# A graph network on one core: places of the edges summed as rows of one bank, in three wide products a group

## The reference

```
def L0(x):                                   # edge_index = [src, dst]
    feat = concat([x[dst], x[src] - x[dst]], -1)
    messages = relu(feat @ W1 + b1) @ W2 + b2
    out = segment_max(messages, dst)         # 0 where a row has no edge
def L1(x):
    h = x + segment_sum(x[src], dst)
    h = relu(h @ W1 + b1) @ W2 + b2
    return x @ Wres + bres + h
x = layernorm(x + L0(x))
x = layernorm(x + L1(x))
```

## Time and profile before

| | |
|---|---|
| median of three runs | 1157.18 us (1156.98 to 1157.43) |
| the profiled execution | 1157.41 us, its span 1155.6 us, mean granted clock 0.981 |
| TensorE products / weight loads | 1083.7 us (94%) / 836.6 us (72%) |
| VectorE, ScalarE, GpSimd | 939.1 (81%), 896.5 (78%), 764.7 us (66%) |
| transfers | 232.04 MB, 201 GB/s over the span |

### The profile page before, as it was taken

One profiled execution on the slowest core, in us unless ns is written; L12 is line 12 of the kernel. 1 busy time (PEld: TensorE's weight loads), 2 busy tenths in 40 slices (PEclk: granted clock), 3 DMA queues, 4 the chain that ended last, 5 costly groups with the idle time before them and its releaser, 6 DMA issues.

```text
span 1155.6 us, 27075 instructions
## 1 busy us (share of the span) xinstructions
PE 1083.7 (94%) x7463; PEld 836.6 (72%) x7463; DVE 939.1 (81%) x3648; ACT 896.5 (78%) x3876; POOL 764.7 (66%) x798
## 2 busy tenths in 40 slices
PE   4699999999999999999979999999999999999992
PEld 3477777776666666666658888888888888888882
DVE  5588988987888888888858778777777799999981
ACT  1578888887888888888867888888888877777772
POOL 6777777777777766662037777777777777777006
PEclk9899999999999999999989999999999999999997
DMA  4578778885787887776566666666655566666532
GB/s 135 173 225 233 238 238 242 240 235 169 196 223 216 219 231 204 216 216 181 169 196 199 211 204 191 210 206 191 206 173 180 182 217 220 215 217 221 180 135 82
DMA packets 172193, 232.04 MB, mean 201 GB/s; under 512 B 25508, under 2 KB 90641, under 8 KB 172044
## 3 DMA queue, kind: packets, MB, share of 16 engines
q1 hardware_dynamic: 145372, 180.84, 49.9%
q0 software_dynamic: 25088, 48.94, 16.8%
q10 hardware_dynamic: 1584, 0.53, 0.2%
HBM read 129.48 MB, written 102.96 MB: 201 GB/s over the span
## 4 chain that ended last, share of the span: by engine, by line
PE 54%; POOL 26%; issue 10%; DVE 7%; DMA 1%; ACT 1%; DVEq 0%; SPq 0%; POOLq 0%; ACTq 0%
POOL edge_rows L507 16%; PE psY L1100 10%; PE psY L1099 10%; PE psH L1108 9%; PE psT L1092 5%; POOL xd_early L507 4%; PE psE L1092 4%; POOL src_bc L507 4%; PE psE L1100 4%; PE psE L1099 4%; PE psE L1251 4%; PE psE L1215 3%; DVE shared L733 3%; DVE shared L744 2%; POOL out L511 1%
## 5 line engine op out<-in xcount | busy, mean ns | idle before, releaser
L1099 PE MATMUL psY<-wc,hT 128*128 128x128 f32 x1568 | 305.9, 277 | 2.6 <-ACT o_rows L948 2.2
L1100 PE MATMUL psY<-wcr,xT 128*128 128x128 f32 x1568 | 305.3, 277 | 0.0
L511 POOL DMA_INDIRECT out<-edge_rows,idx x196 | 195.0, 995 | 116.7 <-DMA out<-o_rows 57.5
L507 POOL DMA_INDIRECT edge_rows<-x1e_table,idx x196 | 189.0, 965 | 124.6 <-DMA x1e_table<-shared 65.1
L923 ACT ACTIVATE junk<-psY 128x128 f32<-128x128 f32 x784 | 209.5, 300 | 50.9 <-PE psY L1100 50.9
L1099 PEld LDWEIGHTS psY<-wc,hT 128*128 128x128 f32 x1568 | 240.7, 194 | 3.9 <-issue 3.9
L1100 PEld LDWEIGHTS psY<-wcr,xT 128*128 128x128 f32 x1568 | 240.4, 194 | 0.0
L507 POOL DMA_INDIRECT edge_rows<-in_x,idx x196 | 190.2, 970 | 66.0 <-issue 59.5
L585 DVE TENSOR_SCALAR x<-x_in,mv,rs 128x128 f32<-128x128 f32 x784 | 220.5, 359 | 0.5
L1108 PE MATMUL psH<-xT,wc 128*128 128x512 f32 x392 | 205.5, 606 | 16.0 <-DVE deltas L664 10.2
L579 DVE BATCH_NORM_STATS2 bn_a<-x_in 128x6 f32<-128x128 f32 x784 | 164.6, 271 | 19.6 <-DMA x_in<-in_x 19.5
(11 more groups left out here) (125 smaller groups left out, 1996.3 us busy)
## 6 DMA issues: line engine op xcount, KB each, us to landing
x_in<-in_x SPq DMA_DIRECT2D x196, 256.0 KB
out<-o_rows SPq DMA_DIRECT2D x196, 256.0 KB
src_bc<-src_dram SPq DMA_DIRECT2D x49, 256.0 KB, 4.9
mask<-mask_dram SPq DMA_DIRECT2D x98, 128.0 KB
x1eT_spill<-x1eT SPq DMA_DIRECT2D x49, 256.0 KB, 2.5
x1e_table<-edge_rows SPq DMA_DIRECT2D x49, 256.0 KB, 3.3
x1e_table<-shared SPq DMA_DIRECT2D x49, 256.0 KB, 3.7
x1eT<-x1eT_spill SPq DMA_DIRECT2D x49, 256.0 KB, 3.1
```

The source lines that it names most:

```text
L507: nc.gpsimd.indirect_dma_start(to, None, table, bass.IndirectOffsetOnAxis(idx[:, what, t:t + 1], 0)).then_inc(landed[n % FLIGHT], 16)
L511: nc.gpsimd.indirect_dma_start(table, bass.IndirectOffsetOnAxis(idx[:, SCAT, t:t + 1], 0), frm, None, bounds_check=limit, oob_is_err=False ...
L1099: t_.matmul(to[:, cut(t)], h[:, cut(t)], wc2[:, :], start=t == 0, stop=False, skip_group_check=True)
L1100: last = t_.matmul(to[:, cut(t)], xt[:, cut(t)], wcr[:, :], start=False, stop=t == TILES - 1, skip_group_check=True)
```

## The change

`place` now swaps the operands. The stationary operand is a window of 128 columns of `place_w`, which is zero but for one or two columns; the moving one is the whole of `match` or `steps` of the group, 512 columns. The window of group g begins at column 96 - 2g, so that its filled columns fall on rows 2g and 2g+1 of the result. All groups add into the one bank psE[2], and each puts its two numbers on two rows of its own. The bank is opened by group 0 and closed by group 48.

There is no copy per group any more. After the search VectorE copies the whole bank to `place_rows`, TensorE transposes it into psE[3] with four transposes, and one copy of VectorE of 4 x 98 columns puts the numbers to `places`, in the old order. `copy_xs(0)` moves ahead of that copy and of the index steps.

```diff
+    PAIR_AT = 2 * GROUPS - 2
+    WINDOW = PAIR_AT + P
-        place_w = sb("place_w", [P, 4], FP16)
+        place_w = sb("place_w", [P, 2, WINDOW], FP16)
+        place_rows = x1eT[:, 1, :]
...
-            def keep_places(g):
-
-                if is_group(g):
-                    dve.wait_ge(pos_done, g + 1)
-                    v.tensor_copy(places[:, g * TILES:(g + 1) * TILES, :],
-                                  psE[2 + g % 2][:, 0:2 * TILES]
-                                  .rearrange("p (n c) -> p n c", c=2)).then_inc(places_done, 1)
...
-                keep_places(s - 3)
 
             def lead_a():
-                dve.wait_ge(places_done, GROUPS)
+                dve.wait_ge(pos_done, GROUPS)
+                v.tensor_copy(place_rows, psE[2][:, :]).then_inc(rows_kept, 1)
+                copy_xs(0)
+                dve.wait_ge(rows_turned, 1)
+                v.tensor_copy(places.rearrange("p (g t) c -> p t g c", t=TILES),
+                              tiles(psE[3][:, :])[:, :, 0:2 * GROUPS]
+                              .rearrange("p t (g c) -> p t g c", c=2)).then_inc(places_done, 1)
+                dve.wait_ge(places_done, 1)
...
-                copy_xs(0)
...
-            v.memset(place_w[:, 1:2], 1.0)
-            v.memset(place_w[:, 2:3], float(P))
-            v.memset(place_w[:, 3:4], 0.0)
+            v.memset(place_w[:, 0, 0:PAIR_AT], 0.0)
+            v.memset(place_w[:, 0, PAIR_AT + 1:PAIR_AT + 2], 1.0)
+            v.memset(place_w[:, 0, PAIR_AT + 2:WINDOW], 0.0)
+            v.memset(place_w[:, 1, 0:PAIR_AT], 0.0)
+            v.memset(place_w[:, 1, PAIR_AT:PAIR_AT + 1], float(P))
+            v.memset(place_w[:, 1, PAIR_AT + 1:WINDOW], 0.0)
...
-            v.tensor_copy(place_w[:, 0:1], row_number[:, :])
+            v.tensor_copy(place_w[:, 0, PAIR_AT:PAIR_AT + 1], row_number[:, :])
...
+                    window = slice(PAIR_AT - 2 * g, PAIR_AT - 2 * g + P)
                     pe.wait_ge(match_done, g + 1)
-                    wait(pe, places_done, g - 1)
-                    for t in range(TILES):
-                        to = psE[2 + q][:, 2 * t:2 * t + 2]
-                        t_.matmul(to, match[:, q, cut(t)], place_w[:, 0:2], start=True, stop=False,
-                                  skip_group_check=True)
-                        t_.matmul(to, steps[:, r, 0, cut(t)], place_w[:, 2:4], start=False, stop=False,
-                                  skip_group_check=True)
-                        last = t_.matmul(to, steps[:, r, 1, cut(t)], place_w[:, 2:4], start=False, stop=True,
-                                         skip_group_check=True)
+                    t_.matmul(psE[2][:, :], place_w[:, 0, window], match[:, q, :], start=g == 0, stop=False,
+                              skip_group_check=True)
+                    for h in range(2):
+                        last = t_.matmul(psE[2][:, :], place_w[:, 1, window], steps[:, r, h, :], start=False,
+                                         stop=g == GROUPS - 1 and h == 1, skip_group_check=True)
...
             def lead_a():
                 pe.wait_ge(match_done, GROUPS)
-                pe.wait_ge(places_done, GROUPS)
                 transpose_in(0)
+                pe.wait_ge(rows_kept, 1)
+                transpose4(psE[3], place_rows, rows_turned)
...
                     pe.wait_ge(zT_done, g + 1)
+                    pe.wait_ge(places_done, 1)
```

More of the change, by code:

```diff
@@ L46, in gnn_program @@
     FLIGHT = 16
+    PAIR_AT = 2 * GROUPS - 2
+    WINDOW = PAIR_AT + P
+    assert 2 * GROUPS <= P
     EARLY = GROUPS // 2 + 1
@@ L176, in gnn_program @@
         pos_done = sem("pos_done")
+        rows_kept = sem("place_rows_kept")
+        rows_turned = sem("place_rows_turned")
         places_done = sem("places_done")
```

## The result

The changed kernel took 1174.2 us in the median (1173.85 to 1174.41) against 1157.31 us of the kernel before: ratio 1.0145, interval 1.0127 to 1.0163. It is 16.9 us slower. Forecast was 1173.9.

The account below looks back on a forecast made before the run. TensorE was taken to fill the search step of 4.25 us without a hole; +0.34 us over 49 groups gives +16.7, other terms 0. 1157.41 + 16.7 = 1174.1, less 0.23 for the median: 1173.9 us, range 1170 to 1177.

Parts of the forecast that it names:

- The step: Search step on TensorE: three wide products (0.645 us) replace twelve small pairs (0.305), +0.34 us a group, +16.7 us over 49.
- The price of an operation is its start-to-start time, not its record or its load: TensorE in the search: an old pair costs 26 ns, a wide product 0.215 us, start to start.
- weight-path rival: TensorE's place block: loads and records set the price, -41 to -42 us, 1116; chance 0.03.
- The index by weight loads: TensorE as a whole: headroom judged by the share of weight loads, by which the change helps; no separate size.
- Faster products: Rival, search place products: they run faster than the candidates, about 1161.5 by the skill's figure; chance 0.03.
- The bank open over 49 groups, the lost copy of VectorE, the six fills: Search and kernel start: open bank costs nothing, dropped 0.12 us copy per group gains nothing, fills cost 0.
- The turn: Between search and next stage: added copies and transposes fit into existing waits, cost 0, VectorE with 0.2 us over.
- GpSimd: Destination gathers after the last match: new wait of 7.6 us, without effect on the kernel's time.
- Partly hidden: Rival, way into the next stage: GpSimd's gathers set it, only their 7.6 us shift counts, 1164.8; chance 0.04.
- Every later stage keeps its length, within 2 us: After the turn: every stage has its old length; over 2 us shorter or longer would refute the prediction.

Follow-up runs that it names:

- experiment 7: The changed kernel with the second steps field holding the sum of both, so two wide place products a group in place of three: 1163.72 us, ratio 1.0059.
- experiment 1: The kernel before with the twelve small place products of a group issued twice, 24 pairs: 1171.86 us, ratio 1.0126.
- experiments 1 to 3: Besides experiment 1, two on the changed kernel: place products cut into 256-column halves, 1174.58 us; place products of groups 1 to 48 on left 256 columns only, 1158.85 us.
- experiment 4: The kernel before with the changed turn alone (bank copy, four more transposes, 4 x 98 copy, earlier edge copy), small place products kept: 1157.01 us, ratio 0.9995.
- experiment 5: The kernel before, with GpSimd waiting for the transposes of group 2 before its destination gathers of group 4: 1157.86 us, ratio 1.0008.
- Experiment 6: The kernel before with eight small place pairs a group in place of twelve, the second steps field holding the sum of both: 1156.92 us, ratio 1.0001.
- experiment 9: The kernel before with GpSimd's order alone changed, destination gathers of groups 4 to 7 before the last four source gathers: 1156.70 us, ratio 0.9996.

## Why the prediction was right

- *The step* (+0.34 us a group, +16.7): right. The place block measured 0.65 and 0.305 us in the traces, one wide product 0.214 us by experiment 7, twelve small pairs 0.30 us by experiment 1.
- *The price of an operation is its start-to-start time, not its record or its load*: right, shown by experiments 1 to 3. The weight-path rival (1116) would have needed 54 ns for an old pair; it was 25. The index by weight loads, which the Trainium skill (Perfetto Trace Analysis, section Identifying the Most-Contended Engine) gives next to one by the arithmetic done, pointed the wrong way here: the loads' busy time fell from 836.6 to 834.6 us and the time rose.
- *Faster products* (the figure of 131 ns in the Trainium skill, TensorE: Matmul & The Clock Gate, section Back-to-back issue gap): wrong for this kernel. Three kinds of 512-column f16 stream (candidates, three and two place products) all ran at 0.215 us.
- *The bank open over 49 groups, the lost copy of VectorE, the six fills*: no cost and no gain, as put. In the search TensorE has no wait in either trace.
- *The turn* (0): right, shown by experiment 4. I gave VectorE 0.2 us to spare, it had 0.45; the copies took 0.64 and 0.57 us where I had taken 0.69.
- *GpSimd* (a new wait of 7.6 us, without effect): the effect right, the size wrong. The wait is there, released by VectorE's match, but it lasts 1.41 us:

```profile
284.46 0.95 POOL L513 DMA_INDIRECT edge_rows<-in_x,idx  x1 [0.30 <-issue]
286.81 0.94 POOL L513 DMA_INDIRECT src_bc<-in_x,idx  x1 [1.41 <-DVE match L657]
```

The match came at 285.86 + 0.68 = 286.5 for my 287.8, the search having begun 1.5 us earlier; and GpSimd was done with its earlier gathers at 285.4, where I had left it at the 279.9 of the kernel before. I took GpSimd's pace to be its own. It is not, see below. It did no harm: TensorE's transposes of group 4 came at 315.7 for my 319, and the last of their four gathers ended at 291.5.
- *Partly hidden* (1164.8): wrong for this change, by experiment 5. But GpSimd's lead in the kernel before is small. Experiment 6 took 11.2 us of lateness and 4.6 us of a shorter search from it, and the last transpose of group 4 was 2.8 us late (299.01 for 296.2), so the lead was some 13 us, an estimate. Experiment 5, whose search ended 0.9 us earlier, used 10 of them. The changed kernel wants the rows 15.3 us later and begins to gather them 6.7 us later, so its lead is longer still. For a change that makes the search shorter this rival is the one that decides.
- *Every later stage keeps its length, within 2 us*: right, 0 and +1.2 us.

## What to carry to other kernels

Where TensorE has no hole, price a change by the starts of its products: swapping operands to turn many narrow products into few wide ones pays only if the streamed columns come to less than the sum of the narrow ones' start-to-start times, here 3 x 0.215 against 12 x 0.025 us. The busy times of the groups added up, the loads' busy time and the count of instructions all pointed the other way. Before shortening a stage that one engine fills, look for the engine beside it that works at its own pace towards the next stage: its lead is what the gain is paid from, and once the lead is used up TensorE can pay twice, with the wait and with a lower clock behind it (3.0 and 1.5 us in experiment 6). Reordering the other engine's queue can restore the lead: it cost nothing in experiment 9.

## What the runs showed of the hardware that was not expected

The pace of GpSimd's gathers in the search hangs on how VectorE's steps fall beside them. Most gathers take 0.94 us and start every 1.25 us, but in the changed kernel, from 80 to 260 us, 39 of the 138 gathers seen take over 1.03 us (before: 16 of 142, all beside the same two operations). All 39 overlap both VectorE's second compare (L648) and the scaling behind it (L591); of the 99 others 20 overlap the scaling and none that compare. In the changed kernel, GpSimd and then VectorE:

```profile
178.56 0.94 POOL L513 DMA_INDIRECT edge_rows<-in_x,idx  x1 [0.30 <-issue]
179.81 1.15 POOL L513 DMA_INDIRECT edge_rows<-in_x,idx  x1 [0.30 <-issue]
```

```profile
179.67 0.47 DVE L648 TENSOR_SCALAR shared<-src_bc,first 128x512 f16<-128x512 f32 x1
180.06 1.10 DVE L591 TENSOR_SCALAR x<-x_in,mv,rs 128x128 f32<-128x128 f32 x4
```

With the compare that adds a second field (experiment 6), slow gathers take 1.35 us. With the same compare in experiment 7, at a step of 4.38 us, none of 145 was slow, though 62 lay beside it and 41 of these beside the scaling too; and in experiment 1, where 56 of 140 were slow, three in ten of these had another compare (L651) at their side. So the overlap alone doesn't decide, the moment does too.

The two engines fall into a fixed phase. In the kernel before the gathers come at the same places of the step again every three steps: ten gathers, one of them slow, 10 x 1.25 + 0.2 = 12.7 us for three steps of 4.25. In the changed kernel it is every two steps, with seven gathers, two of them slow: 7 x 1.25 + 0.4 = 9.2 us for 2 x 4.59. In most of experiment 6 it is every step, with three gathers, one of them slow: 3 x 1.25 + 0.4 = 4.15 us. In experiment 7 seven gathers fill two steps (8.75 us) with none slow. So a small change of the step changes GpSimd's pace and moves its end by up to 11 us. Whether slips of this phase also make the wide spread of experiment 6's runs is not shown.

The Trainium skill (SBUF — State Buffer, section Who interferes with whom) says that a VectorE operation in a two-port mode and a GpSimd operation block each other, whoever issued first going on. The slow gathers, in the changed kernel all beside the two operations named, fit that, though no row shows the mode of an operation; the 41 of experiment 7 that lost nothing show that an overlap of the records is not enough for it. No run took the compare away alone, so that it is the cause is argued, not shown.
